# A graph attention layer on one core: means for isolated rows as a bias of the output copy, and the feature bias through an accumulating DMA

## The reference

```python
h = einsum('bnd,ade->bane', x, W)
th = tanh(h)
attn = einsum('bane,aeo->bano', th, w_src) + swapaxes(einsum('bane,aeo->bano', th, w_dst), 2, 3)
attn = where(attn >= 0, attn, 0.2 * attn)
attn = where(~adj[:, None], -999.0, attn)
attn = softmax(attn, axis=-1)
feat_out = einsum('banm,bame->bane', attn, h) + b
feat_out = elu(heads side by side)
gate = sigmoid(x @ H_w.T + H_b)
x = layernorm(x + gate * feat_out + (1 - gate) * x)
```

## Time and profile before

| | |
|---|---|
| median of three runs | 711.69 us |
| the profiled execution, and its span | 711.58 us, 709.8 us |
| PE busy (matmuls) | 678.0 us, 96% |
| DVE busy | 678.3 us, 96% |
| POOL busy | 601.0 us, 85% |
| ACT busy | 412.4 us, 58% |
| mean granted TensorE clock | 0.99 |

### The profile page before, as it was taken

How to read it: one execution, slowest core, us unless ns; L and a number is a source line. 1 busy time by engine, 2 the same in 40 slices (tenths; PEclk the granted TensorE clock), 3 DMA queues, 4 the chain that set the end, 5 groups by cost and what they waited for, 6 DMA issues and landing times.

```text
span 709.8 us, 12409 instructions
## 1 busy us (share of the span) xinstructions
PE 678.0 (96%) x3327; PEld 376.1 (53%) x3327; DVE 678.3 (96%) x1225; ACT 412.4 (58%) x859; POOL 601.0 (85%) x434
## 2 busy tenths in 40 slices
PE   8899999999999999999999999999999999999882
PEld 5464655546555555555655554564646455554530
DVE  7699999999999999999999999999999999999996
ACT  5324558284664838567383765828476482855673
POOL 2964798998989899898989989899898989988393
PEclk9999999999999999999999999999999999999997
DMA  5253335263352615335261443426244351533402
GB/s 193 101 176 117 101 104 196 66 210 112 130 168 94 203 59 188 112 132 173 94 221 59 148 149 134 163 89 213 84 134 163 111 186 61 169 108 128 161 30 89
DMA packets 47083, 94.55 MB, mean 133 GB/s; under 512 B 2962, under 2 KB 28308, under 8 KB 47060
## 3 DMA queue, kind: packets, MB, share of 16 engines
q1 hardware_dynamic: 38868, 82.08, 35.5%
q10 hardware_dynamic: 8192, 12.19, 4.6%
HBM read 81.28 MB, written 12.98 MB: 133 GB/s over the span
## 4 chain that ended last, share of the span: by engine, by line
PE 72%; ACT 10%; DVE 7%; issue 5%; POOL 4%; DMA 2%; ACTq 0%; DVEq 0%; SPq 0%; POOLq 0%
PE out_T L976 37%; PE hg L898 28%; PE tr L984 4%; DVE ew L743 4%; ACT xT_hi L450 3%; ACT scratch L521 2%; ACT att_T L497 1%; PE hg L959 1%; ACT h_sb L462 1%; DMA xT_in<-in_xT 1%; DMA v_all<-v_rows 1%; DVE ex L778 1%; DVE att L761 1%; PE hg L931 1%; DVE att L772 1%
## 5 line engine op out<-in xcount | busy, mean ns | idle before, releaser
L743 DVE SCALAR_TENSOR_TENSOR ew<-v_all,u,adj 128x512 f32<-128x512 f32 x768 | 526.0, 732 | 0.5 <-DMA v_all<-v_rows 0.5
L976 PE MATMUL out_T<-ew,vals 128*64 128x512 f32 x1536 | 367.6, 602 | 2.7 <-DVE ew L743 2.7
L976 PEld LDWEIGHTS out_T<-ew,vals 128*64 128x64 f32 x1536 | 107.3, 137 | 198.3 <-issue 154.7
L301 POOL TENSOR_TENSOR th_w<-th,score_w 128x768 f32<-128x768 f32 x58 | 107.6, 1855 | 48.0 <-ACT th L458 40.8
L497 ACT ACTIVATE att_T<-out_T,tiny 128x512 f32<-128x512 f32 x96 | 65.8, 685 | 134.7 <-PE out_T L976 134.7
L898 PE MATMUL hg<-w_hi,xT_hi 128*128 128x384 f32 x384 | 99.4, 367 | 8.9 <-ACT h_sb L462 6.5
L898 PEld LDWEIGHTS hg<-w_hi,xT_hi 128*128 128x128 f32 x384 | 61.8, 191 | 50.6 <-issue 47.3
L898 PE MATMUL hg<-w_lo,xT_hi 128*128 128x384 f32 x384 | 88.6, 338 | 0.0
L898 PE MATMUL hg<-w_hi,xT_lo 128*128 128x384 f32 x384 | 87.6, 335 | 0.0
L305 POOL TENSOR_TENSOR th_w<-th_w 128x384 f32<-128x384 f32 x58 | 78.1, 1347 | 4.5
L468 ACT ACTIVATE gate_tanh<-hg 128x384 f32<-128x384 f32 x64 | 31.2, 490 | 78.3 <-PE hg L898 78.3
(11 more groups left out here) (106 smaller groups left out, 734.5 us busy)
## 6 DMA issues: line engine op xcount, KB each, us to landing
v_all<-v_rows SPq DMA_DIRECT2D x96, 512.0 KB, 3.8
xT_in<-in_xT SPq DMA_DIRECT2D x16, 768.0 KB, 4.6
x_in<-in_x SPq DMA_DIRECT2D x15, 768.0 KB, 4.5
out<-y ACTq DMA_DIRECT2D x15, 768.0 KB, 5.3
adj_in<-in_adjT SPq DMA_DIRECT2D x16, 256.0 KB, 4.9
xT_in<-in_x SPq DMA_DIRECT2D x1, 768.0 KB, 6.0
ew<-in_W SPq DMA_DIRECT2D x1, 576.0 KB, 4.2
gate<-in_HwT SPq DMA_DIRECT2D x1, 576.0 KB, 8.0
```

Of the source, the lines that this page charges most:

```text
L301: g.tensor_tensor(th_w[:, c % 2], th[:, c].unsqueeze(1).broadcast_to([P, 2, D]), score_w[:], ALU.mult).then_inc(S["thw_done"], 1)
L743: ve.scalar_tensor_tensor(out=ew[:, (2 * C * j + i) % SLOTS, :], in0=v_all[:, j % VSLOTS, k], scalar=u[:, q, c, h:h + 1], in1=ADJ[c][:], o ...
L976: te.matmul(OUT[VW * k:VW * k + VW, :], vals[:, q, c, h, :], ew[:, t % SLOTS, :], start=(c == 0), stop=(c == C - 1)).then_inc(S["ew_free"], 1)
```

## The change

- The mean, times the tiny number, becomes the bias of `copy_out`. A row with neighbours has a sum of weights so much larger that the bias is lost in rounding; in a row without any it is all there is, and the quotient of mean times tiny by tiny is the mean. For this the tiny number goes up to 2^-90, and the values' weight column is multiplied by 2^60 (`exps` gets one more ACT instruction and two waits on itself). `add_means`, `alone` and `means_alone` go, and with them the additions for the last graph.
- `means` is now three matmuls with one column each (the sums are the weights), and stands ahead of `attend(b, 0)`. ACT copies the twelve pieces of 32 numbers into `out_bias` with four instructions (`out_biases`) ahead of `copy_out(b, 0)`.
- `add_bias` is a DMA that POOL issues, with a sum at the destination; it reads the bias, repeated to 1536 numbers, for every partition. It stands ahead of `subtract_x`. The 1 that POOL had added to the bias row is now the bias of ACT's copy of the features, an Identity in place of a Copy.
- At the end, the last graph's exponential of the middle columns moves ahead of `copy_out(5)`, and DVE's tail is ordered anew.

```diff
@@ GpSimd
-                g.tensor_tensor(h_sb[:]..., h_sb[:]..., bias_row[:]..., ALU.add).then_inc(S["hb_done"], 1)
+                pool.dma_start(h_sb[:].rearrange("p c d -> p (c d)"), bias_rows, accum_op=ALU.add).then_inc(S["add_bias_done"], 16)
...
+                if not last:
+                    add_bias(b + 1)
                 if not first:
                     subtract_x(b - 1)
                     mix(b - 1)
                 if not last:
-                    add_bias(b + 1)
                     add_rows(b + 1, 1 - q)
                     values(b + 1, 1 - q)
@@ ScalarE
-                a.activation(h_sb[:, c], feature_bank(b, c)[:, 0:D], ACT.Copy).then_inc(S["hcopy_done"], 1)
+                a.activation(h_sb[:, c], feature_bank(b, c)[:, 0:D], ACT.Identity, bias=plus1[:, 0:1]).then_inc(S["hcopy_done"], 1)
...
-                a.activation(vals[:, q, :, :, E], d_rel[:], ACT.Exp, scale=ALPHA).then_inc(S["exps_done"], 1)
+                a.activation(s_pos[:], d_rel[:], ACT.Exp, scale=ALPHA).then_inc(S["exps_done"], 1)
+                act.wait_ge(S["exps_done"], NEX * b + 1)
+                a.activation(vals[:, q, :, :, E], s_pos[:], ACT.Copy, scale=LIFT).then_inc(S["exps_done"], 1)
...
+            def out_biases(b):
+                act.wait_ge(S["hm_done"], b + 1)
+                act.wait_ge(S["outT_copied"], HP * b)
+                m = out_bias[:].rearrange("p (i s) -> p i s", s=2)
+                for r in range(4):
+                    rows = slice(VW * (r % 2), VW * (r % 2) + E)
+                    a.activation(m[rows, :, r // 2], mean_ps[E * r:E * r + E, :], ACT.Copy).then_inc(S["out_bias_done"], 1)
...
-                a.activation(att_T[:, j % 2], OUT[:], ACT.Identity, bias=tiny[:, 0:1]).then_inc(S["outT_copied"], 1)
+                if j == 0:
+                    act.wait_ge(S["out_bias_done"], 4 * b + 4)
+                a.activation(att_T[:, j % 2], OUT[:], ACT.Identity, bias=out_bias[:, j:j + 1]).then_inc(S["outT_copied"], 1)
@@ VectorE
-                        ve.tensor_scalar(alone[:], t[:, :, 0, E], TINY, None, ALU.is_le).then_inc(S["alone_done"], 1)
...
-                for c in range(C):
-                    ve.scalar_tensor_tensor(out=att[:, q, c], in0=mean_ps, scalar=alone[:, c:c + 1],
-                                            in1=att[:, q, c], op0=ALU.mult, op1=ALU.add).then_inc(S["att1_done"], 1)
...
-                add_means_late(MIDDLE, HP * B - 1)
+                dve.wait_ge(S["gate1_done"], B)
+                elu_late(0, MIDDLE)
                 dve.wait_ge(S["y_early_done"], 2)
                 statistics(0, EARLY)
                 inverses()
                 quotients()
-                add_means_late(FINAL, HP * B)
-                elu_late(0, MIDDLE)
+                gated(MIDDLE, 1)
                 elu_late(1, FINAL)
+                gated(FINAL, 2)
@@ TensorE
-                te.matmul(mean_ps, mean_w[:, 0:1].broadcast_to([P, P]), hb_tot[:, q], start=True, stop=True).then_inc(S["hm_done"], 1)
+                for i in range(H // 4):
+                    last = te.matmul(mean_ps[:, i:i + 1], hb_tot[:, q, i * P:(i + 1) * P], mean_w[:, 0:1],
+                                     start=True, stop=True)
```

More of the change, by code:

```diff
@@ L15 @@
 EPS = 1e-5
-TINY = 1.2e-38
+TINY = 2.0 ** -90
+LIFT = 2.0 ** 60
 def gat_layernorm(nc, x, xT, adjT, W, HwT, w_rows, bias, H_b, out):
     B, N, D = x.shape
-    E = bias.shape[0]
+    E = bias.shape[1]
     H = D // E
@@ L38, in gat_layernorm @@
     SLOTS = 16
-    SETUP = 13
+    SETUP = 12
     DVE_SETUP = 12
@@ L126, in gat_layernorm @@
         w_gate_in = gate[:, 0:KD]
+        bias_rows = bias.rearrange("(o a) e -> o (a e)", o=1).broadcast_to([P, C * D])
         gate_bias_hi = y[:, 0]
@@ L277, in before @@
                 g.memset(vals[:, 1], 0.0).then_inc(S["pool_setup"], 1)
-                pool.wait_ge(S["ld_rows"], 16)
-                g.tensor_scalar(bias_row[:], bias_row[:], 1.0, 1.0, ALU.mult, ALU.add).then_inc(S["pool_setup"], 1)
                 pool.wait_ge(S["pool_setup"], SETUP)
+                pool.wait_ge(S["hcopy_done"], C)
+                add_bias(0)
                 pool.wait_ge(S["scores"], 1)
-                add_bias(0)
                 for c in range(2):
@@ L607, in x_last_form @@
                 a.activation(x_plus1[:], x_last, ACT.Identity, bias=plus1[:, 0:1]).then_inc(S["x_forms_done"], 1)
-            def means_alone():
-                act.wait_ge(S["hm_done"], B)
-                act.wait_ge(S["alone_done"], B)
-                for c in range(C):
-                    a.activation(mean_last[:, c], mean_ps, ACT.Copy, scale=alone[:, c:c + 1]).then_inc(S["mean_last_done"], 1)
             def exp_early(q):
                 y = y_last[:, :, EARLY]
-                act.wait_ge(S["att_last_done"], 1)
+                act.wait_ge(S["att_done"], HP * (B - 1) + 3)
                 act.wait_ge(S["mixed"], 3 * (B - 1) + 3)
@@ L764, in attended @@
                 return [inverses, quotients]
-            def add_means(b, q):
-                dve.wait_ge(S["att_done"], HP * b + HP)
-                dve.wait_ge(S["hm_done"], b + 1)
-                dve.wait_ge(S["alone_done"], b + 1)
-                for c in range(C):
-                    ve.scalar_tensor_tensor(out=att[:, q, c], in0=mean_ps, scalar=alone[:, c:c + 1],
-                                            in1=att[:, q, c], op0=ALU.mult, op1=ALU.add).then_inc(S["att1_done"], 1)
             def elu(b, q):
@@ L805, in step @@
                     edges(b, q, j, between)
-                    if j == 0 and not first:
-                        add_means(b - 1, 1 - q)
             def after():
@@ L991, in step_last @@
                 gates(b, q, 0, True)
+                means(b, q)
                 attend(b, q, 0)
@@ L1001, in step_last @@
                 attend(b, q, 2)
-                means(b, q)
                 transpose_out(b, 2)
@@ L1073 @@
         "w_rows": np.stack([np.asarray(L0_gnn_w_src), np.asarray(L0_gnn_w_dst)]).reshape(2, D),
-        "bias": np.asarray(L0_gnn_b),
+        "bias": np.tile(np.asarray(L0_gnn_b), (x.shape[1] // 128 * H, 1)),
         "H_b": np.asarray(L0_gnn_H_b),
```

79 lines of the change are left out of this document (36 added, 43 removed).

## The result

The kernel after takes 724.53 us (median of four runs, 722.67 to 727.01) against 712.05 us (711.6 to 713.01) for the kernel before: a ratio of 1.0176, 95% interval [1.0142, 1.0209]. I had predicted 714.4 us with a range of 706 to 721. The sign was right; the size was +12.5 us and not +2.7, and it lies outside the range.

What follows compares the result with a forecast made beforehand. PE and DVE were both taken as full (96% busy), PE setting the pace and waiting for DVE only in `attend(b, 1)`. 711.58 + 3.3 (steps) + 0.4 (start) - 1.0 (end) = 714.3 us, 714.4 against the median; range 706 to 721.

Steps and rivals of the forecast that it cites:

- DVE's relief: Pair 0's reciprocal: 0.26 us a step gained against PE; as rival, earlier edges make the kernel faster, 706.5 us, chance 0.20.
- The elu and POOL: Ahead of edge 7 of pair 1: the elu hangs until POOL's product is through, 2.30 us long instead of 1.75.
- The means on PE: Ahead of `attend(b, 0)`: six small matmuls cost 0.4 us a step, bounds 0.25 and 0.87; leaving the old place gains 0.
- POOL and the DMA: Bias addition: the DMA lands in 7 to 9 us, hidden under the mix; POOL gains 3.5 us less 1 for the issue.
- `normalise` and ACT's list: Up to part 2's tanh: -0.40 us for an earlier start, +0.09 features copy, +0.53 four copies; sum +0.22 a step.
- The sum of a step: End of `attend(b, 1)`: about +0.2 us a step, PE's 0.49 us hidden in 0.93 us of waiting; together +3.3 us.
- two chains: To the end of `attend(b, 1)`: first over ACT and POOL, +0.22 us; second over PE's transposes, 0.49 - 0.26 = +0.23 us.
- The start: Before `attend(0, 0)`: +0.4 us, up to +2 if POOL's row sums are not there in time for the first means.
- The end: After the last step: DVE's 1.95 us addition falls away and its tail is reordered, -1.0 us.
- No change: Rival: ACT's four copies take 0.35 us, so a step grows by only 0.05 us; 712.1 us, chance 0.15.
- The slow DMA: Rival: landing later than 14 us after issue delays `shift` and PE in 13 steps; about 742 us at 16, chance 0.07.
- ACT's long list: Rival: the four copies take 0.95 us with full durations, +0.65 us a step; 720 us, chance 0.11.

Runs made afterwards that it cites:

- e6: Kernel after with the next graph's means between pairs 4 and 5, their four copies behind `copy_out(b, 5)`, and the first means behind `attend(0, 0)`: 708.84 us, ratio 0.9954.
- e1: Kernel before with only the adding DMA and the Identity copy of the features; the means stay as they were: 708.11 us, ratio 0.9941.
- e11: Kernel after with means and copies moved into gaps, and DVE's elu behind edge 7 of pair 1; a repeat measurement: 700.78 us, ratio 0.9852.
- e12: Kernel before with the adding DMA and Identity copy, `add_means` still on DVE, and the elu behind edge 7; a repeat measurement: 700.44 us, ratio 0.9842.
- e8: Kernel after with means and copies moved into gaps, and DVE's elu behind edge 7 of pair 1; first measurement: 701.59 us, ratio 0.9843.
- e10: Kernel after with means between pairs 4 and 5 and the first behind `attend(0, 0)`; the four copies stay ahead of `copy_out(b, 0)`: 720.14 us, ratio 1.0113.
- e5: Kernel after with the means done twice on PE, six one-column matmul instructions in place of three: 733.14 us, ratio 1.0292.
- e3: Kernel after with only the means of graph 0 moved behind `attend(0, 0)`: 720.94 us, ratio 1.0126.
- e2: Kernel after without the DMA: POOL adds the feature bias behind the mix again, with ACT's plain Copy of the features: 727.42 us, ratio 1.0210.
- e4: Kernel after with ACT's four small copies of the means done twice, the extra ones into an unread tile: 729.05 us, ratio 1.0235.
- e7: Kernel after with means and copies moved into gaps, but the feature bias added by POOL again and no DMA: 717.56 us, ratio 1.0064.
- e9: Kernel before with the adding DMA and Identity copy, `add_means` still on DVE, and the elu behind edge 7; first measurement: 705.12 us, ratio 0.9900.

## Why the prediction was wrong

**What bounds the kernel.** Right: PE does, and only through `attend(b, 1)` did it wait for DVE. But the 0.26 us a step that I allowed for DVE's relief were too many: e6 against e1 (41.87, 41.82) and e11 against e12 show it at nothing.

**The elu and POOL.** Right. In after the elu ends at 344.27, POOL's product at 342.66: 1.61 us, as the 1.62 in before. In e12 the elu starts 0.10 us after the product's end and takes 1.75. The Trainium skill (SBUF — State Buffer, section Who interferes with whom) has the one issued second blocked. The trace agrees both ways: in e8 POOL's next sum starts 0.06 to 0.10 us behind the elu in the steady steps and takes 2.53 to 2.56 us, not 1.01, while the elu takes 1.75. In e12 it takes 2.64 us too, but there its recorded start lies 0.01 to 0.03 us ahead of the elu's, a lead too small to tell from these records which was issued first.

**The means on PE: the mis-sized term.** I took 0.4 us, within bounds of 0.25 and 0.87. They lie on PE from 376.30 to 376.95, 0.65 us between the starts; e10 gets 0.55 us back ahead of `attend(b, 0)`, and three matmuls more cost 0.66 us in e5. That the old place gave nothing back was right: PE idles 0.89 us there.

**The copy of the features.** Right: 577 ns for 490, and with it e1's stretch ahead of `attend(b, 0)` grew by 0.10.

**POOL and the DMA.** Right in the main: issue 0.91 us, landing 6.6 us (a little under my 7 to 9, within the bounds), hidden under the mix. The Trainium skill's rule that a reducing DMA is half as fast (Collectives: The Full Stack, section The bandwidth ceiling, where it is said of the steps of a collective) made 9 us as an estimate; measured is 6.6 against 4.7 us for a plain load of that size in the same kernel, a factor of 1.4, and the measurement decides.

**`normalise` and ACT's list.** It starts 0.26 us ahead of the first features matmul now, where it stood 0.40 behind it, so it won more than I gave it. But the four copies with the wait behind them take 0.82 us (337.39 to 338.21; 0.78 on average in e10, where PE is out of the way), not 0.53. `copy_out(b, 0)` comes 6.18 us after that matmul, 5.87 before: +0.31 for my +0.22.

**The sum of a step** failed. I had +0.22 by two chains, and said: "PE's own 0.49 later lies inside the 0.93 of waiting and costs nothing more". Measured: +0.69 ahead of `attend(b, 0)`, -0.23 at `attend(b, 1)`, +0.48 in all. The waiting in the step shown fell from 0.93 to 0.65 us, exactly the 0.65 I had named, but two things were wrong. First, both chains got more than I gave them. PE's is 0.70 us later, not 0.49: 0.55 for the means, and 0.15 because the features of part 1 start later (6.75 us behind the start of `attend(b-1, 5)`, 6.60 before), of which the Identity is 0.1. PE's wait for the features' copy grew by more than that (0.44, 0.49 to 0.71, 0.90, by turns), but the transposes ahead of it start some 0.1 us earlier in every kernel with the DMA, so that part costs nothing. ACT's list got some 0.8 us of copies and not 0.53. Second, PE's lateness is not free: PE was 0.20 us from setting `copy_out(b, 0)` itself (table above), so 0.70 later on PE moves it by 0.50, and with it the tanh, POOL's product, the elu and the end of `attend(b, 1)`. ACT's list alone moves the step by 0.42 (e10). My second chain, with 0.70 in place of 0.49, would have said +0.44. I had looked at the wait that was left and not at what PE's lateness does to that wait's own beginning.

**The start** failed. "The DMA starts some 3 us before the old `add_bias`, so they should be there": the sums were not, and I had put +2 as the most. Measured is +4.4, of which the means are 2.8 and the lower clock of that execution 1.0 (e3). I had looked at when the sums' input would come, not at what POOL does first.

**Steps 0 to 3 and 15.** Summed by me as steady ones. Steps 0 to 3 cost 3.9 us, 2 us over four steady ones, 1.2 of it in step 2 from pair 0 to pair 1 (8.58 us, 7.40 before), where ACT's issue of a store took 2.25 us in place of 0.45:

```profile
120.04 2.25 ACTq L544 DMA_DIRECT2D out<-y  x1
```

It is 0.9 to 2.25 us at its first use in after, e3, e5, e6, e8, e10 and e11, and 0.45 in before, e1, e2, e4, e7, e9 and e12. All of the first have the DMA and the new bias; e4 has them too and does not show it. In e3, where it is 1.02 us, the stretch is as short as before (7.39). Its cause stays open. In the last step the gates' wait cost 1.3 us: I had followed the instructions that moved and not the bank that they share.

**The end**: right, -1.4 for -1.0.

Term by term, the profile of after lies above the forecast by 4.0 us at the start, 3.0 in steps 0 to 3, 2.6 in the ten steady steps and 1.3 in step 15, and below it by 0.8 in step 14 and 0.4 at the end: together 9.7 us.

**The rivals.** DVE's relief: fell. No change: fell. The slow DMA: fell. ACT's long list came nearest with 720 us, by the copies' real 0.8 us; but it was no alternative to the longer means: in after both arrive at `copy_out(b, 0)` together (e10). I priced "long list" and "long means" as cases apart, and the start as a side note, and so left their joint end at 722 to 727 us outside the range.

## What to carry to other kernels

An instruction that fills a wait costs nothing; the same instruction ahead of the next long piece of a full engine can cost nearly its whole length in every step (0.66 us for the means doubled, 0.59 of 0.69 for the copies doubled), so ask of each moved one what gap it left and whether there is one on the other side. Two that delay the same next step from two engines cost it once, and moving only one of them gives nothing. Before a delay is called hidden in a wait, ask whether it also delays the thing that is waited for. An engine that is 96% busy can lose 2 us a step for no gain when what is awaited from it stands behind an instruction that waits for others: moving that one instruction was worth 1% here (e12 against e1, e8 against e6), the relief nothing. The first step and the last are summed apart, with the banks and buffers that the moved instruction shares.

## What the runs showed of the hardware

Six one-column matmuls with 128 x 128 weights take 0.55 to 0.66 us of PE's list, some 0.1 us each. Four transposes with 128 columns each take 0.35 us in after (382.23 to 382.58), 0.09 us each: with one column a matmul was no shorter than with 128. Four ACT copies of 32 x 3 numbers, each 0.16 us long, start 0.18 us apart, and an instruction that waits for the last of them starts 0.82 us after the first. Beside an adding DMA, plain loads take longer to land: `xT_in` 6.5 us in after, 4.6 in before and in e2, `adj_in` 6.8 and 4.9; in the steps nothing waited for them.
